# State-space stage: the scans of ten steps run whole over two PSUM banks

## The reference, cut to what matters

```
dA  = exp(A[d, n] * dt[l, d])
dBu = dt[l, d] * B[l, n] * u[l, d]
h[l] = dA[l] * h[l-1] + dBu[l]           # for each channel d and state n
y[d, l] = sum_n h[l, d, n] * C[l, n]
out = ((y + D * u) * silu(gate)) @ W_out.T
```

## Time and profile before

| | |
|---|---|
| median of 3 runs | 3174.01 us |
| lowest and highest | 3170.85 and 3174.55 us |
| span of the profiled execution | 3175.0 us |
| state-space stage | about 0 to 1750 us of it |
| busy share over the span: PE, DVE, ACT, POOL | 94%, 89%, 76%, 66% |

### The profile page before, as it was taken

One profiled execution on the slowest core, in us unless ns is written; L12 is line 12 of the kernel. 1 busy time (PEld: TensorE's weight loads), 2 busy tenths in 40 slices (PEclk: granted clock), 3 DMA queues, 4 the chain that ended last, 5 costly groups with the idle time before them and its releaser, 6 DMA issues. The chain is left out here.

```text
span 3175.0 us, 47891 instructions
## 1 busy us (share of the span) xinstructions
PE 2991.9 (94%) x16134; PEld 1833.1 (58%) x16134; DVE 2833.2 (89%) x4149; ACT 2419.9 (76%) x4531; POOL 2094.4 (66%) x1207
## 2 busy tenths in 40 slices
PE   7899999999999999999987699999999999799998
PEld 4777677767776777777755244444444444244444
DVE  6999999999999999999998788888888888288887
ACT  4888888888888888888875177777777777577786
POOL 5999999999999999999998234334334334100000
PEclk9999999999999999999998699999999999899999
DMA  4112211222022202220221656655655653221111
GB/s 176 32 46 81 81 49 43 80 81 69 23 80 81 79 13 80 84 81 15 77 96 64 180 163 178 182 181 174 186 181 171 183 180 113 101 77 47 47 41 37
DMA packets 164389, 311.97 MB, mean 98 GB/s; under 512 B 22736, under 2 KB 80208, under 8 KB 164000
## 3 DMA queue, kind: packets, MB, share of 16 engines
q1 hardware_dynamic: 158784, 299.53, 29.6%
q10 hardware_dynamic: 5360, 9.38, 1.0%
HBM read 217.16 MB, written 91.69 MB: 97 GB/s over the span
## 5 line engine op out<-in xcount | busy, mean ns | idle before, releaser
L830 POOL TENSOR_TENSOR bu<-du,bc 128x1024 f32<-128x1024 f32 x512 | 1199.0, 2370 | 32.1 <-DMA bc<-bc_scratch 29.9
L708 ACT ACTIVATE states<-dt,negA 128x256 f32<-128x256 f32 x2048 | 852.8, 463 | 240.2 <-DVE hc L926 229.4
L914 DVE TENSOR_TENSOR_SCAN states<-states,bu 128x512 f32<-128x512 f32 x704 | 821.5, 1212 | 10.5 <-ACT states L708 8.2
L1568 DVE TENSOR_REDUCE mmax<-s_ps 128x1 f32<-128x512 f32 x1024 | 673.0, 686 | 126.1 <-PE s_ps L1288 105.2
L1413 ACT ACTIVATE pt<-s_ps 128x512 f32<-128x512 f32 x1024 | 579.6, 595 | 209.5 <-PE s_ps L1297 203.7
L926 DVE TENSOR_TENSOR hc<-states,bc 128x512 f32<-128x512 f32 x704 | 445.7, 674 | 1.6 <-DMA bc<-bc_scratch 1.6
L1288 PE MATMUL s_ps<-kst,qst 102*128 102x512 bf16 x1024 | 400.5, 393 | 28.6 <-DMA kst<-mask_d 19.3
L526 PEld LDWEIGHTS y_ps<-id_sb,hc 128*128 128x128 f32 x2816 | 330.7, 143 | 122.9 <-DVE hc L926 58.2
L526 PE MATMUL y_ps<-id_sb,hc 128*128 128x128 f32 x2816 | 377.1, 277 | 22.8 <-DVE hc L926 22.8
L1297 PE MATMUL s_ps<-qst,kst 105*128 105x512 bf16 x1024 | 387.4, 382 | 5.8 <-ACT pt L1413 3.9
L839 POOL TENSOR_TENSOR hp<-hp,bc 128x1024 f32<-128x1024 f32 x160 | 379.5, 2372 | 2.8 <-DVE hp L914 1.9
(11 more groups left out here) (172 smaller groups left out, 4170.6 us busy)
## 6 DMA issues: line engine op xcount, KB each, us to landing
bc<-bc_scratch SPq DMA_DIRECT2D x128, 512.0 KB, 5.2
stack_d<-parts SPq DMA_DIRECT2D x180, 256.0 KB, 3.0
qst<-stack_d SPq DMA_DIRECT2D x64, 384.0 KB
kst<-stack_d SPq DMA_DIRECT2D x64, 384.0 KB
x<-xres SPq DMA_DIRECT2D x31, 512.0 KB, 4.8
w_raw<-in_w_ffn SPq DMA_DIRECT2D x48, 256.0 KB, 2.8
w_raw<-in_w_ffn SPq DMA_DIRECT2D x16, 768.0 KB, 7.3
xT_sb<-in_xT SPq DMA_DIRECT2D x16, 512.0 KB, 6.0
```

Of the source, the lines that this page charges most:

```text
L708: a = act.activation(states[:, bank, first:first + SEQ], dt[:, t, :], ACT.Exp, scale=negA[:, t, c * NS + n:c * NS + n + 1])
L830: pool.tensor_tensor(bu[:, buf, :].rearrange("p (n l) -> p n l", n=NS), du[:, t % (2 * GRP):t % (2 * GRP) + 1, :].to_broadcast([P, NS, SEQ ...
L914: dve.tensor_tensor_scan(dst, src, bu[:, BU_OF[k][0], cols], 0.0, ALU.mult, ALU.add).then_inc(scan_done, 1)
L1568: dve.tensor_reduce(mmax[:, u // HG, c:c + 1], s1_ps[:, n % S_BANKS], AX.X, ALU.max).then_inc(s1_free, 1)
```

## The change

For the ten steps whose product is on POOL, DVE waits for the decays of both halves and then runs one scan of 1024 columns over both banks, from the first half's bank on, into `hp`; it raises `scan_done` by 2 at its end. Before, it ran one scan of 512 columns for each half, and raised `scan_done` by 1 after each. The other 22 steps are as they were. The banks of the two halves are neighbours (0 and 1, or 2 and 3) in every step.

```diff
+                if k in POOL_STEPS:
+                    first = bank_of_half(k, 0)
+                    src = states[:, first:first + HALVES, :].rearrange("p a l -> p (a l)")
+                    dve.wait_ge(decay_ready, half_of(b, k, HALVES - 1))
+                    dve.tensor_tensor_scan(hp[:, POOL_STEPS.index(k) % 2, :], src, bu[:, BU_OF[k][0], :], 0.0,
+                                           ALU.mult, ALU.add).then_inc(scan_done, HALVES)
+                    return
                 for half in range(HALVES):
                     cols, src = slice(half * HALF, (half + 1) * HALF), states[:, bank_of_half(k, half), :]
-                    dst = hp[:, POOL_STEPS.index(k) % 2, cols] if k in POOL_STEPS else src
                     dve.wait_ge(decay_ready, half_of(b, k, half))
-                    dve.tensor_tensor_scan(dst, src, bu[:, BU_OF[k][0], cols], 0.0, ALU.mult, ALU.add).then_inc(scan_done, 1)
+                    dve.tensor_tensor_scan(src, src, bu[:, BU_OF[k][0], cols], 0.0, ALU.mult, ALU.add).then_inc(scan_done, 1)
```

## The result

| | before | changed |
|---|---|---|
| median (4 runs each) | 3173.65 us | 3196.74 us |
| lowest and highest | 3170.85 and 3174.55 | 3191.58 and 3197.60 |
| span of the profiled execution | 3175.0 | 3194.5 |

The changed kernel takes 1.0070 of the time before (95% interval 1.0056 to 1.0084): 23 us slower, where 11.4 were forecast. A second measurement beside the experiments gave 1.0073 (1.0058 to 1.0088). The time that counts is 1.8 us longer than the profile's span of the same execution: 3196.31 and 3194.5 for the changed kernel, and the same in every profiled run of the experiments. By that, the execution of the kernel before with the span of 3175.0 took some 3176.8 (an estimate), about 3 us above its median and not 1.0, so the profiles show 19.5 of the 23 us.

The account below looks back on a forecast made before the run. Two loops were taken to bound the state-space stage, POOL's at 104.24 us and another at 104.00; delays of 0.65 and 0.30 make the latter 104.95, +11.4 us in all: 3174.0 + 11.4 = 3185.4 us, range 3176 to 3191.

Parts of the forecast that it names:

- Two loops: State-space stage, later batches: POOL's own work sets 104.24 us a batch, another loop through DVE, ACT and PE 104.00.
- The merge saves 0.06: DVE, ten steps a batch: one scan of 2.27 us replaces a pair of 2.33; 9.6 us in all, nearly all hidden.
- POOL's loop: POOL runs without a break in later batches, so its own work makes the period of 104.24 us.
- the other loop: Round through DVE, ACT and PE, 104.00 us a batch; a delay on it shows once over 0.24.
- Piece A: Steps 6 to 8: ACT's decays of step 8 start 0.69 us later, +0.65 a batch at the sum of step 14.
- Piece B: Steps 28 to 30: late decays of step 30 delay the scan of 31 by 0.36 us, the residual by 0.30.
- The other eight: Late release at steps 0, 4, 10, 14, 16, 20, 22 and 25: costed at 0, at most 0.1 us a batch.
- The loop of 104.00: Loop through DVE, ACT and PE: 104.00 + 0.65 + 0.30 = 104.95 us a batch, over POOL's 104.24.
- the sum: Delays added to the loop: 13 periods of 104.95, +11.06 us to the last batch's start, +11.4 in all.
- more: Rival: small delays of steps 16, 20, 22 uncovered, or slower two-bank scan; up to 0.3 more a batch, 3190 us; chance 0.10.
- What would show it: Signs: 2.27 us scans, periods near 104.95, decays of 8 behind scan of 6, DVE waiting about 0.5, POOL 0.7.

Follow-up runs that it names:

- Experiment 7: Kernel before, all scans in halves, with the product of step 4 on DVE instead of POOL: 3173.01 us, ratio 0.9991.
- experiment 4: Changed kernel with eight scans whole and those of steps 6 and 28 in halves: 3175.19 us, ratio 0.9998 against the kernel before.
- experiment 1: Kernel before, scans still in halves, but `scan_done` raised by 2 only behind the second half in the ten steps: 3198.24 us, ratio 1.0069.
- experiment 3: Changed kernel with only the scan of step 28 whole, all others in halves: 3182.37 us, ratio 1.0022 against the kernel before.
- experiments 2: Changed kernel with only the scan of step 6 whole, all others in halves: 3184.15 us, ratio 1.0027 against the kernel before.
- experiment 8: Kernel before with seven scans whole (0, 10, 14, 16, 20, 22, 25), 6 and 28 in halves, product of step 4 on DVE: 3173.16 us, ratio 0.9994.
- 9: Kernel before, POOL's step 4 product moved to step 5, products of 4 and 14 on DVE; 5, 6, 28 in halves, other six whole: 3173.37 us, ratio 0.9993.

## Why the prediction was right and wrong

**Two loops: right.** Experiment 7 takes POOL's away and leaves 104.02; the first batches of experiment 4 show the other at 103.84.

**The merge saves 0.06: right**, at 0.05 (2.279 against 2.33). That next to none of it reaches the time holds only as long as POOL's loop is the bound: eight merges gave no change in experiment 4, but shortened the other loop from 104.00 to 103.84, and the ten give back 0.25 a batch in the changed kernel (105.06, against 105.31 in experiment 1). That the loss comes from the late release and not from the merge, experiment 1 shows.

By the Trainium skill, VectorE: DVE Perf Modes, section The TRN2 errata, each instruction of VectorE that reads SBUF pays a fixed cost, measured there as about 150 cycles, and a larger tile pays it once; as an estimate from that, a merge would save 0.156 us. Here the pair's 2.33 against the single scan's 2.279 is a third of it, since the second scan of a pair starts before the first has ended (twice 1.203 is 2.41); the measurement decides.

**Piece A, +0.65: mechanism right, size +0.74.** ACT starts the decays of step 8 0.10 behind the scan's end, where I had put 0.03, by the wait of another pair of instructions (927.44 to 927.54).

**Piece B, +0.30: about right in the loop, more by itself.** Alone it gave +0.51 (104.51). Both together without any merge gave +1.31 (experiment 1), close to 0.74 + 0.51; with all ten merges, at full clock, +1.06, of which 0.32 is left for piece B.

**The other eight at 0: right for the time** (experiment 4), while in the changed kernel their merges are part of the 0.25 given back.

**"The loop of 104.00 becomes 104.95": right for as long as the clock holds.** It was 105.06, an error of 0.11, and with PE's idle time filled 105.06 to 105.08 in all batches from the third to the fifteenth. That its median of 3185.98 us lies so near the forecast's 3185.4 is luck in part: it is +9.6 against the runs beside it, and the four matmuls removed a slow stretch of the second batch besides.

**The step that failed** is the one from piece B to the sum: "the residual, for which PE idles 1.73, comes at +0.30. From there PE and ACT hand it on". I moved everything behind the wait by 0.30 and left durations as they were. But the wait grew, from 1.73 to 2.12, and its growth was not free: behind it TensorE's clock was at half for 3.4 us in eleven batches, which puts `yT` 0.63 later. The sum has no term for it, 7.2 us in all, and no rival has it either; "more" reached 3190 by small delays elsewhere, of which experiment 4 shows none in the time.

Why did the wait grow? DVE's and PE's timelines around the product of step 31 and the sum behind it, kernel before, then changed kernel:

```profile
892.50 1.27 DVE L926 TENSOR_TENSOR hc<-states,bc 128x512 f32<-128x512 f32 x2
893.87 1.04 PE L526 MATMUL y_ps<-id_sb,hc 128*128 128x128 f32 x8
```
```profile
902.24 1.27 DVE L932 TENSOR_TENSOR hc<-states,bc 128x512 f32<-128x512 f32 x2
903.13 1.09 PE L526 MATMUL y_ps<-id_sb,hc 128*128 128x128 f32 x8
```

Before, PE still had other work when the product was there, and began its sum 1.37 us behind the product's start; now it begins 0.89 behind it. The delay of piece B holds back DVE's product and residual, but not PE's older work, so it comes nearly whole as idle time of PE: 0.39 (1.73 to 2.12), and 0.44 (to 2.17) with step 28 alone whole, which delays more. This is read from the timelines and was not tried by itself.

The sum again, to the start of the last batch: it came 19.9 us later than before (1643.24 and 1623.38), where 11.7 were forecast. The clock is 11 × 0.65 = 7.2 of that. The other terms are the loop at 1.06 instead of 0.95, 13 × 0.11 = 1.4 more, the first two batches, +0.9 instead of +1.6, and the very first scan, which came 0.25 later. The last batch gave back 2.3 instead of 0.3, so that the end of the last scan lies 17.6 later (1738.00 and 1755.59), where 11.4 were forecast. From there to the end of the span it is 1437.0 us before and 1438.9 in the changed kernel, 1.9 more; in the profiles of all these kernels this part, whose code is the same, lasts 1434.2 to 1440.9 with no relation to the edits that I could see. That makes the span 19.5 longer. The medians differ by 23.1, some 3.6 more: by the estimate in the section on the result the profiled execution of the kernel before was 3.2 above its median, and that of the changed kernel was 0.4 below. So the 11.7 us between forecast and measurement are the clock's 7.2 and 1.4 - 0.7 + 0.25 - 2.0 + 1.9 + 3.6 of the rest, and the last two of these are spread between executions as far as the runs tell.

**What would show it, as forecast:** the scan of 2.28; the decays of 8 behind the scan of 6; DVE's wait of 0.56 at step 31. The periods near 104.95 came in the third and fourth batch only (105.06 to 105.08). POOL's wait was forecast for DVE at 0.7 and came for ACT's `dt` at 1.4: `dt` lies behind the same late decays, which I had not followed to POOL. It changes nothing, as POOL is no longer the bound.

**What stays open** is why the same wait of 2.06, 2.12 or 2.17 us costs the clock in some batches and not in others. It depends on the exact timing in some way: with the period at 105.31 it was every other batch, in the changed kernel every one from the fifth to the fifteenth in one profile and to the fourteenth in the other, in experiment 3 five of thirteen. Which path sets the loop at 103.83 is open too.

The Trainium skill, TensorE: Matmul & The Clock Gate, Part 1, says that the monitor that gates the clock runs free of the kernel's start. Unequal ends of equal waits, as these traces have them, would fit that, but no run here shows the monitor itself.

## What to carry to other kernels

Merging two instructions also merges two releases: before counting what the fixed cost saves, find who waits for the first half. Here 0.05 us were saved a merge, and up to 0.7 us of lead taken from ACT at each of ten steps, of which only two mattered; splitting just them (experiment 4) makes the change harmless. When a delay lengthens an idle time of PE that recurs, price not only the delay but a stretch at half clock behind it, and test that by putting worthless matmuls into the gap, few enough to fit.

## What the runs showed of the hardware

- An idle time of PE of 1.69 to 1.75 us ahead of the same matmuls was never followed by the lower clock from the third to the fifteenth batch of the kernel before and of experiments 2, 4 and 7. One of 2.12 to 2.17 us was in some batches, and one of 2.06 us once in experiment 8 and not in 9: 3.4 us at half clock, 0.62 to 0.72 us of the period each time (0.94 with the scans in halves and the late release).
- Four matmuls that nobody reads, 1.89 us of PE's time in that gap, took the changed kernel from 3198.5 to 3186.0 us; 8.5 us of it lie before the end of the last scan in the profiles.
- A float32 matmul of 256 columns is two instructions of about 0.22 us: eight took 3.62 us.
- A scan over two PSUM banks costs nothing extra: 2.28 us for 1024 columns, 2.33 for two scans of 512 columns back to back, 1.20 for one.
